# Mamba-style layer with a mixture of experts: prologue by halves, first spread from two queues, ffn split ahead of the steps

## The reference

```python
x = x + s6(_layernorm(x))       # x: 32 sequences, 256 tokens, 128 wide
x = x + moe(_layernorm(x))

# s6
uo = x @ W_in.T; u, o = uo[..., :256], uo[..., 256:]
u = silu(causal_conv(u, conv_w, taps=4) + conv_b)
g = u @ W_gate.T; delta_lo, b, c = g[:64], g[64:80], g[80:96]   # of the last axis
delta = softplus(delta_lo @ W_delta.T + delta_bias)
h_t = exp(-exp(A_log) * delta_t) * h_{t-1} + delta_t * u_t * b_t    # 256 channels x 16 states
y_t = sum_s h_t[s] * c_t[s] + D * u_t
out = (y * sigmoid(o) * o) @ W_out.T

# moe: 8 experts of width 176, the two best per token with weights scaled to 2.5, and a shared one of 352
y = sum_e combine[e] * (silu(x @ w_gate[e]) * (x @ w_up[e])) @ w_down[e]
out = y + (silu(x @ sw_gate) * (x @ sw_up)) @ sw_down
```

## Time and profile before

| | us |
|---|---|
| runs, median (lowest to highest) | 1152.74 (1152.53 to 1155.55) |
| profiled execution, its own time | 1155.91 |
| its span in the profile | 1154.1 |

### The profile page before, as it was taken

How to read it: one execution, slowest core, us unless ns; L and a number is a source line. 1 busy time by engine, 2 the same in 40 slices (tenths; PEclk the granted TensorE clock), 3 DMA queues, 4 the chain that set the end, 5 groups by cost and what they waited for, 6 DMA issues and landing times.

```text
span 1154.1 us, 25028 instructions
## 1 busy us (share of the span) xinstructions
PE 1069.2 (93%) x8947; PEld 906.1 (79%) x8947; DVE 1051.9 (91%) x1510; ACT 1070.0 (93%) x2177; POOL 1047.6 (91%) x374
## 2 busy tenths in 40 slices
PE   4658999999999999999999999999999999998897
PEld 4436788888888888888888888888888888886786
DVE  4467999999999999999999999999999999999953
ACT  5779999999999999999999999999999999999852
POOL 3699899999999999999999999999999999999810
PEclk9567999999999999999999999999999999999999
DMA  7444444433444443334444433344444333443000
GB/s 187 110 104 112 98 121 109 105 90 89 114 116 103 121 102 106 90 94 111 120 104 121 102 100 86 103 112 110 113 121 102 92 89 104 112 99 96 6 6 10
DMA packets 71478, 115.01 MB, mean 100 GB/s; under 512 B 8173, under 2 KB 30394, under 8 KB 71354
## 3 DMA queue, kind: packets, MB, share of 16 engines
q1 hardware_dynamic: 71354, 113.42, 38.3%
HBM read 41.04 MB, written 5.24 MB: 40 GB/s over the span
## 4 chain that ended last, share of the span: by engine, by line
ACT 53%; PE 28%; issue 12%; DVE 4%; SPq 1%; DMA 1%; POOL 1%; ACTq 0%; DVEq 0%; POOLq 0%
ACT decay_ps L529 20%; PE work_ps L1023 8%; ACT g_silu L516 7%; PE work_ps L1106 6%; PE work_ps L1115 4%; PE acc_ps L1067 4%; ACT L644 3%; ACT L636 3%; ACT L678 3%; ACT L629 3%; PE acc_ps L1143 3%; ACT L697 3%; DVE features L771 2%; ACT xn L550 2%; ACT work_ps L608 2%
## 5 line engine op out<-in xcount | busy, mean ns | idle before, releaser
L437 POOL TENSOR_TENSOR inject<-rep,bc 128x2048 f32<-128x2048 f32 x128 | 581.4, 4566 | 6.2 <-DMA rep<-dd 6.2
L451 POOL TENSOR_TENSOR read<-state,bc 128x1024 f32<-128x1024 f32 x192 | 457.8, 2394 | 25.6 <-DVE state L749 22.0
L749 DVE TENSOR_TENSOR_SCAN state<-decay_ps,inject 128x1024 f32<-128x1024 f32 x192 | 438.2, 2283 | 13.5 <-ACT decay_ps L529 13.5
L529 ACT ACTIVATE decay_ps<-rep,neg_a 128x255 f32<-128x255 f32 x1024 | 426.5, 465 | 3.9 <-DVE decay_ps L764 2.2
L1143 PE MATMUL acc_ps<-ffn_down,features 128*128 128x128 f32 (+1 forms) x1792 | 235.8, 275 | 2.0 <-DVE features L779 2.0
L1143 PEld LDWEIGHTS acc_ps<-ffn_down,features 128*128 128x128 f32 (+1 forms) x1792 | 220.8, 191 | 4.9 <-DVE features L779 2.6
L1115 PE MATMUL work_ps<-xn2T_part,ffn_up 128*128 128x256 f32 x1344 | 203.6, 291 | 10.9 <-ACT g_silu L516 9.6
L1106 PEld LDWEIGHTS work_ps<-xn2T_part,ffn_gate 128*128 128x128 f32 x1344 | 171.4, 190 | 45.4 <-issue 24.7
L1106 PE MATMUL work_ps<-xn2T_part,ffn_gate 128*128 128x256 f32 x1344 | 199.8, 293 | 5.5 <-DVE features L771 5.5
L1115 PEld LDWEIGHTS work_ps<-xn2T_part,ffn_up 128*128 128x128 f32 x1344 | 173.0, 190 | 34.8 <-ACT g_silu L516 24.1
L771 DVE TENSOR_TENSOR features<-g_silu,work_ps 128x512 f32<-128x512 f32 x224 | 152.6, 681 | 25.1 <-PE work_ps L1115 22.7
(11 more groups left out here) (136 smaller groups left out, 1244.3 us busy)
## 6 DMA issues: line engine op xcount, KB each, us to landing
rep<-dd SPq DMA_DIRECT2D x256, 256.0 KB, 4.8
bc<-bc_rows SPq DMA_DIRECT2D x64, 512.0 KB, 3.9
x_in<-in_L_attn_x_dram SPq DMA_DIRECT2D x32, 128.0 KB, 2.2
out_dram<-result SPq DMA_DIRECT2D x32, 128.0 KB, 1.9
bc_rows<-g_sb SPq DMA_DIRECT2D x32, 32.0 KB
state<-in_L_ffn_w_gate_dram SPq DMA_DIRECT2D x1, 704.0 KB, 4.4
inject<-in_L_ffn_w_up_dram SPq DMA_DIRECT2D x1, 704.0 KB, 5.9
ffn_down<-in_L_ffn_w_down_dram SPq DMA_DIRECT2D x1, 704.0 KB, 7.4
```

What stands on the lines that cost most here:

```text
L437: pool.tensor_tensor(inject[:, slot:slot + many], du_all, b_all, ALU.mult).then_inc(inject_done, many)
L451: pool.tensor_tensor(read[:, slot:slot + many], state[:, first:first + many], c_all, ALU.mult).then_inc(read_done, many)
L529: last = act.activation(decay_ps[:, at % 2, j, 1:T], rep[(HALVES * n + half) % RP][:, j, 0, 1:T], ACT.Exp, scale=neg_a[:, col:col + 1])
L749: dve.tensor_tensor_scan(to, decays, inject[:, at % RI].rearrange("p j t -> p (j t)"), 0.0, ALU.mult, ALU.add).then_inc(state_done, 1)
```

## The change

It reorders and splits the prologue and touches three places of the body.

- TensorE turns the convolution's weights by halves with turn_xn(0) between, convolves the first half before it turns the other weights (turn_gates), and turns wo, wout and the router's weights after project_z(0) (turn_outs).
- ACT casts the high part of the convolution's weights (copy_conv), DVE keeps the subtraction. ACT's copies are split into copy_gates and copy_outs; softplus of sequence 0 goes directly to dd in two halves, DVE multiplies by u half by half.
- SP issues two of the four rep transfers of half 0 as soon as the first half of dd is there, ACT issues the other two (first_spread); half 1 goes ahead of the c rows.
- DVE's copy of csel and the split of the ffn weights move from step -1 into the prologue, behind the products with u and ahead of the router, the wo subtractions, the clearing of decay_ps and all steps.
- One table load of ACT in step -1 is removed. ACT's wait for silu_done in the body gets the extra condition later(1), which leaves it out in the steps 31 to 33; a wait of DVE gets its own condition twice. copy_z and copy_delta count one less on delta_done, since sequence 0 no longer raises it.

```diff
@@ -383,11 +386,12 @@
             rows_out(0)
             sp.wait_ge(bc_out, 16)
             spread_rows(0, 0, b_in)
+            sp.wait_ge(first_du, 1)
+            spread_half(0, 0, JB // 2)
             sp.wait_ge(dd_done, 1)
             sp.wait_ge(du_done, 1)
-            spread_half(0, 0)
+            spread_half(0, 1)
             spread_rows(0, 1, c_in)
-            spread_half(0, 1)
 
             def body(k, on, later):
                 if on(-3):
...
             shifts(-4)
-            pool.wait_ge(turned, 1)
+            pool.wait_ge(turned, 2)
...
 
         @block.scalar
         def _(act):
-            def copy_weights():
-                act.wait_ge(turned, 2)
+            def copy_conv(half):
+                act.wait_ge(turned, half + 1)
+                act.copy(wconv[0][:, half, :, :].rearrange("d k h -> d (k h)"), turned_ps[:, half, :]).then_inc(conv_high, 1)
+
+            def copy_gates():
+                act.wait_ge(turned, 3)
                 for half in range(HALVES):
-                    cols = slice(half * P, (half + 1) * P)
                     act.copy(wg[:, half, :], turned_ps[:, 3, half * P:half * P + GATES]).then_inc(act_weights, 1)
                     act.copy(wdelta[0:RANK, half, :],
                              turned_ps[0:RANK, 3, (2 + half) * P:(3 + half) * P]).then_inc(act_weights, 1)
+                act.wait_ge(weights_ready, 2)
+                act.activation(neg_a[:], turned_a, ACT.Exp).then_inc(prep_a, 1)
+
+            def copy_outs():
+                act.wait_ge(turned, 4)
+                for half in range(HALVES):
+                    cols = slice(half * P, (half + 1) * P)
                     act.copy(wo[0][:, half, :], turned_ps[:, 2, cols]).then_inc(act_weights, 1)
                     act.copy(wout[:, half, :], turned_ps[:, 2, (2 + half) * P:(3 + half) * P]).then_inc(act_weights, 1)
 
-                act.wait_ge(weights_ready, EARLY_WEIGHTS)
-                act.activation(neg_a[:], turned_a, ACT.Exp).then_inc(prep_a, 1)
+            def first_spread():
+                act.wait_ge(first_du, 1)
+                for j in range(JB // 2, JB):
+                    source = dd[j * CB:(j + 1) * CB, 0, :, :].rearrange("c w t -> c (w t)")
+                    act.dma_start(rep[0][:, j, :, :].rearrange("p w t -> p (w t)"),
+                                  source.unsqueeze(1).broadcast_to([CB, GS, 2 * T])).then_inc(rep_in[0], 16)
 
             def silu(n, p):
                 at = PAIRS * n + p
...
-                if on(-2):
+                if on(-2) and later(1):
...
                     decays(k, 4)
                 if k == -1:
                     act.wait_ge(weights_ready, WEIGHTS)
-                    act.preload_act_table_set("natural_log_exp_and_others")
                     decays(0, 0)
                     decays(0, 1)
                 if later(2) or on(-2):
...
             log_vars(-4)
             rstds(-4)
             norm1(0)
+            copy_conv(0)
             xn_high(0)
+            copy_conv(1)
             xn_low(0)
-            copy_weights()
+            copy_gates()
             act.preload_act_table_set("silu_and_others")
-            act.wait_ge(weights_ready, EARLY_WEIGHTS)
+            act.wait_ge(weights_ready, 1)
             conv_silu(0)
             copy_g(0)
             act.preload_act_table_set("softplus")
             act.wait_ge(z_mm, 1)
-            act.activation(delta_ps, z_ps, ACT.Softplus).then_inc(delta_done, 1)
-            act.wait_ge(delta_done, 1)
-            act.copy(dd[:, :, 0, :], delta_ps).then_inc(dd_done, 1)
+            act.activation(dd[:, 0, 0, :], z_ps[:, 0, :], ACT.Softplus).then_inc(first_delta, 1)
+            act.activation(dd[:, 1, 0, :], z_ps[:, 1, :], ACT.Softplus).then_inc(dd_done, 1)
+            first_spread()
+            copy_outs()
             steps(body)
 
         @block.vector
...
                                   ALU.subtract).then_inc(comb_split, 1)
 
             def body(k, on, later):
-                if k == -1:
-                    dve.wait_ge(consts, 4)
...
-                    dve.tensor_tensor(ffn_gate[1][:], gate_staged, ffn_gate[0][:].bitcast(F32),
-                                      ALU.subtract).then_inc(ffn_ready, 1)
-                    dve.tensor_tensor(ffn_up[1][:], up_staged, ffn_up[0][:].bitcast(F32),
-                                      ALU.subtract).then_inc(ffn_ready, 1)
-                    dve.wait_ge(ffn_ready, PARTS)
                 if on(0):
                     scan(k, 0)
...
-                if on(-2):
+                if on(-2) and on(-2):
...
             dve.wait_ge(prep, PARTS + 2)
             stats_x(0)
+            dve.wait_ge(consts, 1)
+            dve.tensor_scalar(neg_identr[:], ident[:], -1.0, None, ALU.mult).then_inc(neg_ready, 1)
             dve.wait_ge(conv_loaded, 16 * len(conv_loads))
             for half in range(HALVES):
                 for tap in range(TAPS):
                     dve.tensor_scalar(wconv_rows[:, half, tap, :], win_rows[:, half, :],
                                       taps[:, half, tap:tap + 1], None, ALU.mult).then_inc(prep, 1)
-            dve.wait_ge(consts, 1)
-            dve.tensor_scalar(neg_identr[:], ident[:], -1.0, None, ALU.mult).then_inc(neg_ready, 1)
-            dve.wait_ge(turned, 1)
             for half in range(HALVES):
-                dve.tensor_copy(wconv[0][:, half, :, :].rearrange("d k h -> d (k h)"),
-                                turned_ps[:, half, :]).then_inc(conv_ready, 1)
-            dve.wait_ge(conv_ready, HALVES)
-            for half in range(HALVES):
+                dve.wait_ge(conv_high, half + 1)
                 dve.tensor_tensor(wconv[1][:, half, :, :].rearrange("d k h -> d (k h)"), turned_ps[:, half, :],
                                   wconv[0][:, half, :, :].rearrange("d k h -> d (k h)").bitcast(F32),
                                   ALU.subtract).then_inc(conv_ready, 1)
-            dve.wait_ge(turned, 2)
+            dve.wait_ge(turned, 3)
             dve.tensor_copy(conv_bias[:], turned_vectors[:, 0:HALVES]).then_inc(weights_ready, 1)
             dve.tensor_copy(skip_d[:], turned_vectors[:, HALVES:]).then_inc(weights_ready, 1)
-            dve.tensor_copy(router[:], banks[0][:, 0:EXPERTS]).then_inc(weights_ready, 1)
-            dve.tensor_copy(router_parts[0][:], banks[0][:, 0:EXPERTS]).then_inc(weights_ready, 1)
-            dve.wait_ge(weights_ready, EARLY_WEIGHTS)
-            dve.tensor_tensor(router_parts[1][:], router[:], router_parts[0][:].bitcast(F32),
-                              ALU.subtract).then_inc(weights_ready, 1)
+            dve.wait_ge(weights_ready, 2)
             for half in range(HALVES):
                 dve.tensor_scalar(skip[:, half, :], ident[:], skip_d[:, half:half + 1], None,
                                   ALU.mult).then_inc(weights_ready, 1)
             dve.wait_ge(prep_a, 1)
             dve.tensor_scalar(neg_a[:], neg_a[:], -1.0, None, ALU.mult).then_inc(weights_ready, 1)
+            dve.wait_ge(first_delta, 1)
+            dve.tensor_tensor(dd[:, 0, 1, :], dd[:, 0, 0, :], u[0][:, 0, :], ALU.mult).then_inc(first_du, 1)
+            dve.wait_ge(dd_done, 1)
+            dve.tensor_tensor(dd[:, 1, 1, :], dd[:, 1, 0, :], u[0][:, 1, :], ALU.mult).then_inc(du_done, 1)
+            dve.wait_ge(consts, 4)
+            dve.tensor_copy(csel[:], csel_rows).then_inc(csel_ready, 1)
+            dve.wait_ge(ffn_loaded, 16 * len(ffn_loads))
+            dve.wait_ge(padded, 2)
+            dve.tensor_copy(ffn_gate[0][:], gate_staged).then_inc(ffn_high, 1)
+            dve.tensor_copy(ffn_up[0][:], up_staged).then_inc(ffn_high, 1)
+            dve.wait_ge(ffn_high, PARTS)
+            dve.tensor_tensor(ffn_gate[1][:], gate_staged, ffn_gate[0][:].bitcast(F32),
+                              ALU.subtract).then_inc(ffn_ready, 1)
+            dve.tensor_tensor(ffn_up[1][:], up_staged, ffn_up[0][:].bitcast(F32),
+                              ALU.subtract).then_inc(ffn_ready, 1)
+            dve.wait_ge(ffn_ready, PARTS)
+            dve.wait_ge(turned, 4)
+            dve.tensor_copy(router[:], turned_router).then_inc(weights_ready, 1)
+            dve.tensor_copy(router_parts[0][:], turned_router).then_inc(weights_ready, 1)
+            dve.wait_ge(weights_ready, WEIGHTS - 1 - HALVES)
+            dve.tensor_tensor(router_parts[1][:], router[:], router_parts[0][:].bitcast(F32),
+                              ALU.subtract).then_inc(weights_ready, 1)
             dve.wait_ge(act_weights, ACT_WEIGHTS)
             for half in range(HALVES):
                 dve.tensor_tensor(wo[1][:, half, :], turned_ps[:, 2, half * P:(half + 1) * P],
...
-            dve.wait_ge(dd_done, 1)
-            dve.tensor_tensor(dd[:, :, 1, :], delta_ps, u[0][:], ALU.mult).then_inc(du_done, 1)
...
-            def turn_conv():
+            def turn_conv(half):
```

(28 more changed lines are left out.)

24 lines of the change are left out of this document (8 added, 16 removed).

## The result

| | median us (lowest to highest) | runs | ratio to before, 95% |
|---|---|---|---|
| before | 1154.22 (1152.27 to 1155.55) | 12 | |
| changed | 1156.78 (1154.57 to 1157.82) | 12 | 1.0021 (1.0012 to 1.0029) |

The change costs 2.4 us (0.21%, by the ratio); the forecast was +1.3, within 0.3%. The changed kernel's profiled execution took 1157.17, its span is 1155.3, 1.2 more than before's. The nine runs of before that came to the first three raised its median from 1152.74 to 1154.22, so the forecast of 1154.0 for the changed kernel's median is compared by its difference.

A forecast was written before the change was run, and what follows sets the result against it. Entry into the packed steps, set by ACT's copy of z of sequence 1, bounds the kernel; the first scan's 4.6 us delay shrinks to +1.3 there, giving 1154.0 on the median (1157.2 profiled), range 1151.5 to 1157.3.

The forecast's parts named there:

- Part 1: Prologue by halves ahead of the first dd: u of sequence 1's predecessor 1.7 us earlier, dd and du complete at 20.25, -2.5.
- Part 2: Spread of rep split between SP and ACT: ACT's two transfers cost 1.3 us, covered; half 0 lands at 25 to 26.
- Part 3: Ffn split in DVE's prologue delays sequence 1's stats; log_var at 28.6 (+5.3), first injection at 29.6, only 0.9 earlier.
- Part 4: ACT's second table load removed: 0.7 of its 1.3 us realised; first scan at 41.75, 4.6 later than before.
- Part 5: Extra wait conditions on ACT and DVE: nothing, at most 0.3 us in three places with lost overlap.
- What of it reaches the end: Of the first scan's 4.6 us delay, +1.3 reaches ACT's copy of z; +0.9 or +2.8 by TensorE's clock.
- what moves 43.48 moves the rest: ACT's copy of z of sequence 1, at 43.48 before, sets the entry into the packed steady steps and so the end.
- rival 1: Slower: the earlier prologue work meets TensorE still at 1.2 GHz, +3.1 or +4.6 us; chance 0.17.
- rival 2: The start of POOL's injections sets everything: -0.9 us, 1151.8; chance 0.09.
- 3: Faster: POOL's injections start when rep lands (25.5), -5.0 us, 1147.7; needs DVE's stats ahead of the ffn split; chance 0.08.
- the nearer case of rival 1: Cold TensorE slows sequence 0's projections, with the z copy of sequence 1 as forecast: +3.1 us.

## Why the prediction was right, point by point

**Part 1.** du was complete at 20.47 (forecast 20.25). The path was another one than worked out: the convolution ended at 14.8 by the faster level, and ACT's table load, until 15.50, set u at 15.52.

**Part 2.** The two transfers took ACT 1.29 (taken: 1.3), with 5.2 us of idle time behind as cover. The landing of half 0 was forecast for 25 to 26 and was at 28.5 to 28.8 in the kernels in which POOL waited for it. That step was wrong: the b rows are issued only at 21.00, and the DMA engines are busy with both until 28. It changed nothing in the sum, as said. Issuing from two engines moved the landing by 1.4 us (28.56 against 29.94), which is about the 1.29 that ACT's issue took; so the rule of the Trainium skill (DMA: Bandwidth & Descriptors, Issuing engines are not separate DMA queues) that was set against this part came nearer than the part.

**Part 3.** The split ended at 27.3 (27.1), stats at 28.25 (28.1), log_var at 28.78 (28.6), the first injection at 29.74 (29.6), and moving the stats alone gave 2.2 parts in a thousand back. What the step missed is the gain: with the split out of the way POOL's two injections take 0.4 us less.

**Part 4.** u at 40.75 (40.85), first scan at 41.62 (41.75), the load worth 0.8 (0.7).

**Part 5.** No run takes the two conditions back, so that they cost nothing is not shown.

**What of it reaches the end.** z was copied at 44.49, +1.0 (taken +1.3, bounds +0.9 and +2.8), with both projections at 2.4 GHz. The gate product behind it, at the same level, won another 0.5, so that the steps were entered 0.5 late. At the other level, in the run with the load put back, the entry came at 57.27.

**The size.** Measured +2.4 (1.4 to 3.3) against +1.3. What failed is the step "what moves 43.48 moves the rest". Of the 1.0 us at z only 0.5 reached the entry, and behind it the four waits of DVE add 1.4, for which the sum has no term. That makes 0.5 + 1.4 from the traces, or 2.7 with the forecast's +1.3; both are in the interval. In the two traces the distance is 0.5 at 55 us, 0.3 at 121, 1.5 at 1049 and 1.2 at the end. The forecast of 1157.2 for the profiled execution, measured 1157.17, is therefore luck: an entry taken 0.8 too late, four waits of 1.4 taken at nothing, and 0.7 that the trace gives back elsewhere happen to cancel. Which part of the rest is TensorE's level in executions that have no trace stays open.

**Rivals.** 1, the cold array: project_g of sequence 0 took 1.07, TensorE had risen by then. 2 fell by the split moved alone. 3 needed the stats ahead of the split; with them there the kernel is 2.2 parts in a thousand faster than changed and level with before, not 5 us below it, since rep lands at 28.6 and the late weights hold ACT. The chances don't all fit the prices beside them: +3.1, the nearer case of rival 1, lies within 0.3% but most of that rival's chance stands under slower, and rival 2, at -0.9, has 0.02 there.

## What to carry to other kernels

Before work is moved ahead of a loop, list what stands behind it on its engine: here a 0.4 us instruction behind a 6.9 us block fed three engines, and putting it first turned a loss of 2.4 us into none. Look also at what the block runs beside: a block that is hidden on its own engine can still block another one. And where a change is worth one part in a thousand, the steady steps have to be compared too, since one place more or less in DVE's list decides over four waits that add 1.4 us.

## What was not expected of the hardware

DVE's own issue stops it for about 0.3 us at one place of its list and again every 640 instructions, eight steps, if a scan stands exactly there: four times in each of the eight traces in which that scan is the 192nd instruction, never in the six in which it is the 191st, the 193rd or the 200th. Why it stops there was not tried. POOL stands still during DVE's subtraction of two SBUF operands: 1.84 of 1.97 us, 0.92 of 1.05, 0.83 of 0.95 and 0.40 of 0.53 for the multiplications, and 1.16 of 1.29 for the small shift of the kernel with the stats first (24.18 us, 1.36 instead of 0.20), each time 0.12 or 0.13 less than the overlap. TensorE's level in the first 120 us differs between executions of one program; the runs of each kernel spread by about 3 us, and filling its gaps up to 45 us did not narrow that. And the first matmuls of the convolution go at the lower level's pace (twelve in 2.90 us, where half of the 24 at 85.28 in the earlier trace rows, at a granted clock of 0.50, make 2.73) although the column of the granted clock shows 1.00 there.
